# Gelu through Tanh and a polynomial on the vector engine in a cross-attention megakernel on one core

## The reference

```python
scores = qk / math.sqrt(dk)                      # 16 heads, 64 x 1601
feats = jnp.stack([mean_sim, max_sim, entropy_proxy], axis=-1)      # per head
hidden = jax.nn.gelu(_linear(feats, w1, b1), approximate=False)     # 3 -> 64
hidden = jax.nn.gelu(_linear(hidden, w2, b2), approximate=False)    # 64 -> 64
log_t = jnp.clip(_linear(hidden, w3, b3), LOG_T_MIN, LOG_T_MAX)     # 64 -> 1
t = jnp.exp(log_t)[..., None]
attn = jax.nn.softmax(qk / (2.0 * t), axis=-1)
```

## Time and profile before

| what | value |
|---|---|
| time, three runs | 1216.24, 1218.23, 1223.19 us |
| median | 1218.23 us |
| span of the profiled execution | 1213.1 us (its time outside the span is not given) |
| PE busy | 1101.5 us, 91% |
| DVE busy | 812.4 us, 67% |
| ACT busy | 765.5 us, 63% |
| POOL busy | 406.0 us, 33% |
| chain of work that ended last | PE 75%, DVE 12%, issue 5%, ACT 4% |

### The profile page before, as it was taken

How to read it: one execution, slowest core, us unless ns; L and a number is a source line. 1 busy time by engine, 2 the same in 40 slices (tenths; PEclk the granted TensorE clock), 3 DMA queues, 4 the chain that set the end, 5 groups by cost and what they waited for, 6 DMA issues and landing times.

```text
span 1213.1 us, 39205 instructions
## 1 busy us (share of the span) xinstructions
PE 1101.5 (91%) x14964; PEld 892.8 (74%) x14964; DVE 812.4 (67%) x2128; ACT 765.5 (63%) x1547; POOL 406.0 (33%) x420
## 2 busy tenths in 40 slices
PE   3867799999999999999999999999999999999864
PEld 3535587878888787878878797878787887867743
DVE  4467667566776776677777776577667777578245
ACT  2434576776766676767766776667767676766521
POOL 2268352223232331433232332333143233331223
PEclk9968798987979897989999898989889898989787
DMA  4610010201010111102010111102020100000000
GB/s 132 193 29 27 23 37 4 61 11 42 19 44 21 36 29 28 37 2 54 11 45 20 37 29 29 36 4 61 2 54 11 45 20 19 3 2 6 8 2 9
DMA packets 46812, 38.85 MB, mean 32 GB/s; under 512 B 14576, under 2 KB 46000, under 8 KB 46640
## 3 DMA queue, kind: packets, MB, share of 16 engines
q1 hardware_dynamic: 46640, 36.41, 11.1%
HBM read 34.30 MB, written 2.10 MB: 30 GB/s over the span
## 4 chain that ended last, share of the span: by engine, by line
PE 75%; DVE 12%; issue 5%; ACT 4%; DMA 2%; POOL 1%; SPq 1%; DVEq 0%; ACTq 0%; POOLq 0%
PE pjp L665 14%; PE s1p L704 14%; PE s2p L735 13%; PE pjp L658 12%; PE pvp L752 8%; DVE est L1392 3%; DVE negm L1386 2%; PE tlp L848 2%; PE tlp L866 1%; PE tlp L787 1%; ACT ering L1045 1%; PE tlp L842 1%; PE s2p L725 1%; PE s2p L645 1%; PE tlp L809 1%
## 5 line engine op out<-in xcount | busy, mean ns | idle before, releaser
L1386 DVE TENSOR_REDUCE negm<-s1p 128x1 f32<-128x400 f32 (+1 forms) x512 | 289.8, 566 | 199.1 <-PE s1p L704 196.6
L1045 ACT ACTIVATE ering<-s1p,negm 128x400 f32<-128x400 f32 (+1 forms) x512 | 303.8, 597 | 118.6 <-DVE negm L1386 112.2
L1056 ACT ACTIVATE pring<-s2p 128x512 f32<-128x512 f32 x427 | 240.8, 565 | 148.1 <-PE s2p L735 145.1
L704 PE MATMUL s1p<-kt,qbd 32*128 32x400 f32 (+1 forms) x1024 | 305.2, 608 | 28.1 <-ACT ering L1045 26.1
L1392 DVE BATCH_NORM_STATS2 est<-ering 128x6 f32<-128x400 f32 (+1 forms) x512 | 290.7, 568 | 19.6 <-ACT ering L1045 19.6
L735 PE MATMUL s2p<-q2bd,kt 32*128 32x128 f32 (+1 forms) x3192 | 244.6, 285 | 0.0
L735 PEld LDWEIGHTS s2p<-q2bd,kt 32*128 32x128 f32 (+1 forms) x3192 | 233.3, 194 | 5.8
L658 PE MATMUL pjp<-cr,wkv 128*128 128x256 f32 (+1 forms) x1344 | 192.4, 295 | 29.7 <-DVE vt L1358 19.2
L1264 POOL TENSOR_TENSOR cr<-stage,cr 128x512 fp32r<-128x512 f32 (+1 forms) x112 | 132.1, 1180 | 234.3 <-ACT cr L1036 234.3
L658 PEld LDWEIGHTS pjp<-cr,wkv 128*128 128x128 f32 x1344 | 171.8, 198 | 45.5 <-issue 29.1
L665 PE MATMUL pjp<-wkv,cr 128*128 128x256 f32 (+1 forms) x1200 | 195.7, 318 | 10.0 <-ACT kt L1018 9.8
(11 more groups left out here) (278 smaller groups left out, 1033.1 us busy)
## 6 DMA issues: line engine op xcount, KB each, us to landing
stage<-in_ctx SPq DMA_DIRECT2D x96, 256.0 KB, 3.0
qbd<-q_dram SPq DMA_DIRECT2D x128, 8.0 KB, 1.8
stage<-in_ctx SPq DMA_DIRECT2D x16, 65.0 KB, 2.5
vt<-in_x SPq DMA_DIRECT2D x1, 1024.0 KB, 6.8
q_dram<-late SPq DMA_DIRECT2D x1, 1024.0 KB, 4.6
late<-in_x SPq DMA_DIRECT2D x7, 128.0 KB, 2.3
out_y<-late SPq DMA_DIRECT2D x7, 128.0 KB, 1.8
late<-in_gate SPq DMA_DIRECT2D x1, 768.0 KB, 4.9
```

The lines of the kernel that those rows point to most:

```text
L704: nc.tensor.matmul(s1p[u % 3][:, 0:w], qbd[s.par][rows, g, :], kt[s.par][rows, g, lo:lo + w], start=True, stop=True).then_inc(s1_full, 1)
L1045: nc.scalar.activation(ering[:, u % 3, 0:w], s1p[u % 3][:, 0:w], ACT.Exp, bias=negm[s.par][:, p, c:c + 1]).then_inc(s1_exp, 1)
L1056: nc.scalar.activation(ring_place(s, v)[0:m, 0:n], s2_bank(s, v)[0:m, 0:n], ACT.Exp).then_inc(s2_exp, 1)
L1386: nc.vector.tensor_reduce(negm[s.par][:, p, ch:ch + 1], s1p[u % 3][:, 0:w], AX.X, ALU.max, negate=True).then_inc(s1_max, 1)
```

## The change

The two Gelus no longer use ACT's Gelu. DVE computes half of the pre-activation, its square and a polynomial in it (seven coefficients, `ERF_R`), nine chained instructions in all (`gelu` part 0, `GE_N` = 9), which keep two intermediate results in `tlp`; ACT takes a Tanh of the result (`gelu_tanh`), and DVE multiplies (part 1). Tanh is used elsewhere in the loop beside Exp without a table load, so no table load is needed in the loop. Part 0 stands ahead of the maximum of steps 6 and 8 on DVE, part 1 behind it; the Tanh stands on ACT in steps 6 and 8 ahead of the first-pass exponential. Layers 0, 1 and 2 are now at steps 5, 7 and 9 of PE, after `project`, so `values` of step 6 comes before layer 1. Statistics parts 2 and 3 move from steps 8 and 10 to 9 and 11, the exponential of the temperature from step 9 to 10, and unit 23's exponential goes back to its place at step 6. Hidden values have 128 rows instead of 64: the weights are widened with zeros, which three small memsets on POOL write at the start.

```diff
-STATS_AT = [1, 3, 8, 10]
-MLP_AT = {5: 0, 6: 1, 7: 2}
+STATS_AT = [1, 3, 9, 11]
+MLP_AT = {5: 0, 7: 1, 9: 2}
-W_AT, GELU_AT, C_AT = 2, 5, 9
+W_AT, C_AT = 2, 10
+GELU_AT = [6, 8]
+HALF_R = [2.0 * 2.0 ** k * c for k, c in enumerate(ERF_R)]
+GE_N = len(HALF_R) + 2
...
-                        mm = nc.tensor.matmul(tlp[0:DH, 0:H], w1m[:, f, :], fm[:, f, :, :].rearrange("p i h -> p (i h)"),
+                        mm = nc.tensor.matmul(tlp[:, 0:H], w1m[:, f, :], fm[:, f, :, :].rearrange("p i h -> p (i h)"),
...
-                        if step in MLP_AT and s.has(1, B):
-                            temperature(s, MLP_AT[step])
...
-            def gelu(s, n):
-                need(act, mlp_full, s.lin(N_MLP, n + 1 - N_MLP))
-                nc.scalar.activation(hid[:, n, :], tlp[0:DH, 0:H], ACT.Gelu,
-                                     bias=col("b1" if n == 0 else "b2", 0, DH)).then_inc(mlp_free, 1)
+            def gelu_tanh(s, n):
+                need(act, ge, s.lin(2 * GE_N, GE_N * (n + 1) - 2 * GE_N))
+                nc.scalar.activation(tlp[:, H:2 * H], gy[:, :], ACT.Tanh).then_inc(ge_th, 1)
...
-                    if s.has(1, B) and step == GELU_AT + 1:
-                        gelu(s, 1)
...
+                    if s.has(1, B) and step in GELU_AT:
+                        gelu_tanh(s, GELU_AT.index(step))
                     s_, u = s.unit(step, 1)
                     if s_.has(0, B - 1):
                         exp1(s_, u)
...
-                    if step == GELU_AT and s.prev().has(1, B):
-                        exp2(s.prev(), S2_EARLY)
-                    if s.has(1, B) and step == GELU_AT:
-                        gelu(s, 0)
...
+            nc.gpsimd.memset(w1m[:, :, DH:P], 0.0).then_inc(w_zero, 1)
...
+            def gelu(s, n, part):
+                x, b = gx[:, n, :], col("b1" if n == 0 else "b2")
+                q, low = tlp[:, H:2 * H], tlp[:, 2 * H:3 * H]
+                if part == 0:
+                    need(dve, mlp_full, s.lin(N_MLP, n + 1 - N_MLP))
+                    c = Chain(ge, s.lin(2 * GE_N, GE_N * n - 2 * GE_N))
+                    c(nc.vector.tensor_scalar(x, tlp[:, 0:H], b, 0.5, ALU.add, ALU.mult))
+                    c(nc.vector.scalar_tensor_tensor(out=q, in0=tlp[:, 0:H], scalar=b, in1=x, op0=ALU.add, op1=ALU.mult))
+                    c(nc.vector.tensor_scalar(gu[:, :], q, HALF_R[-1], HALF_R[-2], ALU.mult, ALU.add))
+                    c(nc.vector.tensor_tensor(gu[:, :], gu[:, :], q, ALU.mult))
+                    for r in HALF_R[-3:0:-1]:
+                        c(nc.vector.scalar_tensor_tensor(out=low if r == HALF_R[1] else gu[:, :], in0=gu[:, :], scalar=r,
+                                                         in1=q, op0=ALU.add, op1=ALU.mult))
+                    c(nc.vector.scalar_tensor_tensor(out=gy[:, :], in0=low, scalar=HALF_R[0], in1=x, op0=ALU.add,
+                                                     op1=ALU.mult), False)
+                else:
+                    need(dve, ge_th, s.lin(2, n + 1 - 2))
+                    nc.vector.scalar_tensor_tensor(out=hid[:, n, :], in0=q, scalar=1.0, in1=x, op0=ALU.add,
+                                                   op1=ALU.mult).then_inc(mlp_free, 1)
...
                 for step in range(STEPS):
+                    if s.has(1, B) and step in GELU_AT:
+                        gelu(s, GELU_AT.index(step), 0)
                     if s.has(0, B - 1):
                         maxima(s, step)
+                    if s.has(1, B) and step in GELU_AT:
+                        gelu(s, GELU_AT.index(step), 1)
```

More of the change, by code:

```diff
@@ L77 @@
 S2_AT = [s for s in range(14, 14 + S2U + 2) if s not in S2_IDLE]
-S2_EARLY = S2_AT.index(STEPS + 5)
 S1_P = [0, 1, 2, 3, 4, 5, 6, 7, 2, 3, 0, 1, 4, 5, 6, 7] + 2 * list(range(NPAIR))
-STATS_AT = [1, 3, 8, 10]
-MLP_AT = {5: 0, 6: 1, 7: 2}
+STATS_AT = [1, 3, 9, 11]
+MLP_AT = {5: 0, 7: 1, 9: 2}
 N_MLP = len(MLP_AT)
-W_AT, GELU_AT, C_AT = 2, 5, 9
+W_AT, C_AT = 2, 10
+GELU_AT = [6, 8]
 FIN_AT = [14, 15]
+ERF_R = [7.97884216e-01, 3.63342834e-02, -3.31298998e-05, -5.52401877e-05, 3.96911353e-06, -1.33446665e-07,
+         1.80562219e-09]
+HALF_R = [2.0 * 2.0 ** k * c for k, c in enumerate(ERF_R)]
+GE_N = len(HALF_R) + 2
 QUERIES_AT = 22
@@ L292, in build @@
         wkv = sb("wkv", [P, 2, 2, DB, D], F32R)
-        w1m = sb("w1m", [P, 3, DH])
+        w1m = sb("w1m", [P, 3, P])
         fm = sb("fm", [P, 3, 2, NPAIR])
-        w2s = sb("w2s", [DH, P])
-        w3b = sb("w3b", [DH, P])
+        w2s = sb("w2s", [P, P])
+        w3b = sb("w3b", [P, P])
         wi, wg2, wout = (sb(n, [P, DB, D]) for n in ("wi", "wg2", "wout"))
@@ L345, in build @@
         hm = sb("hm", [P, DB, H])
-        hid = sb("hid", [DH, 2, H])
+        hid = sb("hid", [P, 2, H])
+        gu = sb("gu", [P, H])
+        gy = sb("gy", [P, H])
+        gx = sb("gx", [P, 2, H])
         lt = sb("lt", [P, 3, H])
@@ L429, in build @@
         mlp_full, mlp_free = sem("mlp_full"), sem("mlp_free")
+        ge, ge_th = sem("ge"), sem("ge_th")
+        w_zero = sem("w_zero")
         sc = sem("sc")
@@ L537, in _ @@
                 load_context(w, slice(0, 1))
-            for w, n in ((blockmask, "blockmask"), (w2s, "w2"), (w3b, "w3b")):
+            for w, n in ((blockmask[:, :], "blockmask"), (w2s[0:DH, :], "w2"), (w3b[0:DH, :], "w3b")):
                 sp.dma_start(w[:, :], t[n]).then_inc(consts_in, 16)
@@ L682, in temperature @@
                         pe.wait_ge(wt_out, len(W_SLOT[1]))
+                    if s.b == 1:
+                        pe.wait_ge(w_zero, 3)
                     for f in range(3):
-                        mm = nc.tensor.matmul(tlp[0:DH, 0:H], w1m[:, f, :], fm[:, f, :, :].rearrange("p i h -> p (i h)"),
+                        mm = nc.tensor.matmul(tlp[:, 0:H], w1m[:, f, :], fm[:, f, :, :].rearrange("p i h -> p (i h)"),
                                               start=(f == 0), stop=(f == 2))
@@ L1124, in slot @@
                     s_, v = s.second(step, 1)
-                    if s_.has(1, B) and v < S2U and not s_.drains() and v != S2_EARLY:
+                    if s_.has(1, B) and v < S2U and not s_.drains():
                         exp2(s_, v)
@@ L1198, in _ @@
             nc.gpsimd.memset(powh[:, :], -0.5)
+            nc.gpsimd.memset(w1m[:, :, DH:P], 0.0).then_inc(w_zero, 1)
+            pool.wait_ge(w_zero, 1)
+            nc.gpsimd.memset(w2s[DH:P, :], 0.0).then_inc(w_zero, 1)
+            pool.wait_ge(w_zero, 2)
+            nc.gpsimd.memset(w3b[DH:P, :], 0.0).then_inc(w_zero, 1)
+            pool.wait_ge(w_zero, 3)
             nc.gpsimd.memset(epst[:, :], EPS).then_inc(setup_pool, 1)
@@ L1364, in _ @@
             for f, k in enumerate((1.0 / (SQ * SK), -1.0 / SQ, 1.0 / SQ)):
-                c(nc.vector.tensor_scalar(w1m[:, f, :], w1b[:, f, :], k, None, ALU.mult), False)
+                c(nc.vector.tensor_scalar(w1m[:, f, 0:DH], w1b[:, f, :], k, None, ALU.mult), False)
             bk = cols[:, COL["bk"][0]:COL["bk"][0] + DB]
@@ L1461, in statistics @@
                     assert SC_CLIP + c.n == SC_N
+            def gelu(s, n, part):
[13 more added lines that the diff above has]
+                                                     op1=ALU.mult), False)
+                    assert c.n == GE_N
+                else:
+                    need(dve, ge_th, s.lin(2, n + 1 - 2))
+                    nc.vector.scalar_tensor_tensor(out=hid[:, n, :], in0=q, scalar=1.0, in1=x, op0=ALU.add,
+                                                   op1=ALU.mult).then_inc(mlp_free, 1)
             def key_column(s, what):
```

## The result

The changed kernel takes 1269.4 us (median of 4 runs, 1258.5 to 1274.4), the kernel before 1220.7 beside it: a ratio of 1.039, 95% interval 1.033 to 1.045. It is slower, as forecast, but by 49 us where 13 were forecast, and outside the range.

What follows compares the result with a forecast made beforehand. PE was taken as the bound, except in steps 6 to 13, where it waits and runs at half clock. 14 slots x 0.75 = 10.5 us plus 2.5 in the last slot gave +13: median 1231 us, range 1206 to 1248.

Steps and rivals of the forecast that it cites:

- The chain: Nine chained DVE instructions for each Gelu were to take 1.9 us.
- rival (a): DVE's chain is dearer, up to 3.4 us, because PSUM is written and read back: 1255 us, half of it 1243; chance 0.15.
- Layer 0: First small layer on PE: weights of 128 columns instead of 64 make six weight loads 0.3 us longer.
- The scores of step 8: On PE, in slots with r = 2, they were to start 3.9 to 4.0 us after layer 0.
- The nine instructions take just the place that the two table loads leave: First Gelu, both kinds of slot: DVE's chain replaces ACT's loads in time, so the gain is nothing, within 0.1 us.
- The last slot: No scores cover anything there: layer 0 to unit 26's second-pass scores goes from 5.9 to 8.4 us, 2.5 more.
- Layers 1 and 2 on PE: Layer 2 and the row behind it, before step 10's scores, delay step 11's projection by 0.75 us a slot, 10.5 in all.
- nothing, within 0.1 us: Gain forecast at the first Gelu, up to the scores of step 8, in slots of both kinds.
- I therefore leave the half clock where it is: PE's wait at the first Gelu does not shrink, so the time at half clock was taken as unchanged.
- Rival (b): The longer single wait in slots with r = 1 keeps the clock down 3.3 us longer: 20 us more, 1251; chance 0.08.
- (d): Values before the wait, layer 1 and step 8 right behind it shorten the half clock: say 1200 us; chance 0.14.
- (e): ACT gains more than the loads' rows, step 8 starts without a wait: at most 19 us less, 1212; chance 0.03.

Runs made afterwards that it cites:

- e3: Kernel before with Tanh on ACT in place of Gelu in both layers: no table loads, no DVE chain, old order; 1181.0 us.
- e10: Changed kernel with the last key block (steps 11 and 12) projected at full width, surplus columns unused; 1224.3 us.
- e8: Kernel before with two unused ACT instructions of 0.63 us each ahead of a slot's first Gelu, making PE's wait longer; 1218.7 us.
- e6: Changed kernel without DVE's chain: one Tanh on ACT, straight from PSUM, as the whole Gelu, new order kept; 1202.3 us.
- e14: e6 with the last key block projected at full width; 1160.4 us.
- e15: e3 with the last key block projected at full width; 1179.0 us.
- e19: e14 with four unused ACT instructions of 0.63 us ahead of the first Tanh, making PE wait without work on DVE; 1227.9 us.
- e1: Changed kernel with four extra unused matmuls behind the values of step 6, where PE waits for the first Gelu; 1257.9 us.

## Why the prediction was right or wrong

**Right.** The chain: 1.89 us for 1.9; PSUM written and read back on DVE costs 0.03 us a time at most, so rival (a) is out. Layer 0 takes 0.73 us where it took 0.52: 0.2 more, for 0.3. The scores of step 8: 3.91 us after layer 0, 3.9 to 4.0 forecast. DVE 60 us busier for 58. PE idles once, before layer 1, ended by DVE: 1.18 us where about 1.45 was forecast, and 2.73 in the slots of the earlier trace rows for 2.8. "The nine instructions take just the place that the two table loads leave": yes; e3 and the chain's price below say what that place is worth. The last slot: from layer 0 (1174.20) to the scores of unit 26 (1182.90) 8.7 us, for 8.4 against 5.9 before.

**Two terms that made up for each other.** Layers 1 and 2 on PE were to cost 0.75 us a slot, all of it between the projection of step 9 and that of step 11. The rows of a slot with r = 1, the first two before and the others after:

```profile
530.44 0.49 PE L684 MATMUL tlp<-fm,w1m 128*64 128x16 f32 x6 [0.33 <-DVE fm L1432]
538.89 2.93 PE L665 MATMUL pjp<-wkv,cr 128*128 128x256 f32 x12
...
537.73 0.81 PE L699 MATMUL tlp<-fm,w1m 128*128 128x16 f32 x6 [0.30 <-DVE fm L1446]
542.89 0.40 PE L702 MATMUL tlp<-hid,w2s 128*128 128x16 f32 x2 [2.73 <-DVE hid L1495]
545.68 2.93 PE L678 MATMUL pjp<-wkv,cr 128*128 128x256 f32 x12
551.78 2.77 PE L671 MATMUL pjp<-cr,wkv 128*128 128x66 f32 x12
```

Between the two projections it was 4.87 us (543.76 - 538.89) and is 6.10; with r = 2 it was 5.57 and is 5.95. That is 1.23 and 0.38 more, 0.8 on average: the term was right. But from layer 0 to the projection of step 9 the slot became shorter, from 8.45 to 7.95 us and from 6.59 to 6.16, where I had "nothing, within 0.1 us". Layer 0 to the projection of step 11 is thus 14.05 us for 13.32 with r = 1, and 12.11 for 12.16 with r = 2: about 5 us in 14 slots, for 10.5. These are one slot of each kind, so the sizes are rough.

**The step that failed** is "I therefore leave the half clock where it is". It put 112 us of half clock at nothing. I had priced the clock by the length of the first fall alone, and never asked what follows it. The wait did stay (35.0 us before, 36.4 after), and in the slot of the earlier trace rows so did the first fall (6.8 us). But the half clock reached into and past the last key block's work at steps 11 and 12: a second fall grew from 3.5 us in that slot to 17.1 (such falls were up to 10.2 us in other slots with r = 2 before), and in a slot with r = 1 one stretch grew from 10.2 to 17.1. e10 shows what this costs: 45 us, against 5 in the kernel before, so 40 of the 49 us. Rival (b) had the sign and the kind (a longer half clock, in the slots with r = 1 as it said) but another cause, and 20 us. e8 speaks against its cause, and so does e10, whose wait is as long and whose half clock in those slots is mostly back at 6.8 us.

**Which part of the change does what** can be read from a square of four kernels that all have the order after:

| order after | thin | wide |
|---|---|---|
| Tanh straight on ACT | 1202.3 (e6) | 1160.4 (e14) |
| with the chain | 1269.4 | 1224.3 (e10) |

The chain costs 67 us with the thin work and 64 without, the thin work 45 and 42: they add up, so the second fall does not hang on the chain's wait. With the order before, thin work costs 2 to 5 us (1181.0 to 1179.0 with Tanh, 1218.8 to 1214.1 with Gelu). So the change, from the kernel before on, is: loads gone, -38 (e3); order and weights, with the thin work, +21 (e6); chain, +67; in all +50, as it must be, since the steps lead from the one kernel to the other. With the block wide the same steps are -35 (e15), -19 (e14) and +64 (e10), in all +10. That this is near the forecast's 13 is luck: the forecast had none of the three. The loss that a wide last block undoes was made by the new order and the thin work together, and the loads' gain was given back by the chain's wait at the same place.

What is it in the order that lengthens the second fall? The wider weights of layers 0 to 2, layer 2 behind the projection of step 9, or the statistics a step later were not tried one by one. That stays open.

**Rivals (d) and (e)** expected gains that lie elsewhere than I put them. Removing the loads gained 38 us (e3), by a wait and a clock fall that go with them. The Trainium skill (ScalarE: Activation LUTs, What ACT_TABLE_LOAD costs) would put it down to a drain of about 1380 ns beside each load. No run here shows one: in the kernel before the loads' groups have 0.6 us of idle time in all, and the load at 596.55 ends at 597.83 with the Gelu behind it at 597.84. What e3 shows instead is that PE's waits at layer 1 and at the scores of step 8 fell from 8.9 and 26.1 us to 0.4 and 7.3, and the half clock by 52 us.

## What to carry to other kernels

Where the clock is part of the time, price a wait not by its length but by whether it is the one that brings the clock down: one of 1.5 to 2.0 us a slot cost 67 us here where there had been none (e19), and about a microsecond more a slot cost nothing where PE waited already (e8). Look at the mean clock times the span first, cut the windows where the clock changes, and look for the stretch that stands in or behind small matmuls and not only behind a wait. And try a thin tail at full width: 0.15 us a slot of more columns bought 45 us in the new order, though only 2 to 5 in the old one.

## What the runs showed of the hardware

The granted clock can fall and stay at half while PE is busy without a gap: it fell within 619.20:622.60, where PE is busy for 3.40 of 3.40 us, and at 622.60:639.70 PE is busy for 17.10 of 17.10 us at 0.51, through full projections of 128x256, and comes back only then. The Trainium skill (TensorE: Matmul & The Clock Gate, Part 1) has the clock go by how busy TensorE has been; the waits in e19 agree with it (0.70 behind 1.49 us), this stretch doesn't if busy means that matmuls run. With the same block at 256 columns and 128 weights it did not happen, though PE was hardly longer busy.

A matmul of `ident` and `wo` over 256 columns stands as two instructions in the trace of e1, 31.7 / 60 = 0.53 us for one, against 1.65 / 12 = 0.14 us for one of the same shape in a projection, whose weights are of another type (`wkv`, F32R). Two chained DVE instructions that pass their result through PSUM started 0.21 us apart in the changed kernel (610.89 and 611.10), and 0.28 where the first has a column as its scalar (609.58 and 609.86). Through SBUF it was 0.20 (610.07 and 610.27) and 0.27 (609.31 and 609.58).
